# Sixteen-head causal attention: the diagonal mask moves from matmuls on TensorE to additions on VectorE

## The reference, cut to what matters

```python
q = x @ Wq;  k, v = split(x @ Wkv)             # (2, 16 heads, 1024, 16)
s = (q * 16**-0.5) @ k.T                       # (2, 16, 1024, 1024)
s = where(causal, s, very_negative)            # key <= query
out = softmax(s, axis=-1) @ v @ Wo
```

## Time and profile before

| | |
|---|---|
| time, median of 3 runs | 3386.32 us (3378.21 to 3391.15) |
| profiled execution, its own time | 3392.3 us |
| its span, first to last instruction | 3390.5 us |
| TensorE (matmul) busy | 3055.6 us, 90% |
| VectorE busy | 1947.1 us, 57% |
| ScalarE busy | 1551.8 us, 46% |
| mean granted TensorE clock | 0.944 of full speed |

### The profile page before, as it was taken

The page is one execution under the profiler, slowest core; times in us unless marked ns, Lnnn a source line. Parts: engine busy times, 40 slices in busy tenths (PEclk is TensorE's granted clock), DMA queues, the critical chain, the costliest instruction groups (busy, mean ns, idle before and its releaser), DMA issues. The chain is left out here.

```text
span 3390.5 us, 50330 instructions
## 1 busy us (share of the span) xinstructions
PE 3055.6 (90%) x17338; PEld 2117.3 (62%) x17338; DVE 1947.1 (57%) x4655; ACT 1551.8 (46%) x3708; POOL 289.9 (9%) x605
## 2 busy tenths in 40 slices
PE   7999799989999999855879999997999999959996
PEld 5555566654677777533457777775477777736764
DVE  3556455535676765785757777535477677442223
ACT  1110355542666664454446666524266666313332
POOL 0003000000011110000000000000011111002222
PEclk8998899989999999886989999998999999979998
DMA  1007433127344441010542222102734444341112
GB/s 39 19 14 161 52 47 47 14 74 222 114 140 130 145 134 46 1 29 2 156 121 80 70 82 69 41 2 74 222 117 148 120 144 136 117 145 34 33 34 90
DMA packets 233450, 293.70 MB, mean 87 GB/s; under 512 B 25502, under 2 KB 178334, under 8 KB 233073
## 3 DMA queue, kind: packets, MB, share of 16 engines
q1 hardware_dynamic: 229466, 280.39, 29.8%
q0 software_dynamic: 3744, 10.23, 1.0%
HBM read 222.01 MB, written 68.10 MB: 86 GB/s over the span
## 5 line engine op out<-in xcount | busy, mean ns | idle before, releaser
L2076 ACT ACTIVATE cond_p<-cond_p,cond_negm 128x128 f32<-128x128 f32 (+7 forms) x768 | 593.1, 775 | 419.9 <-DVE cond_negm L2107 419.2
L2057 PE MATMUL ps_o<-cond_pt,cond_v 128*64 128x256 f32 (+1 forms) x3840 | 480.5, 371 | 5.2 <-DVE attn_out L2143 0.5
L2035 PE MATMUL ps_s<-cond_k_high,cond_q_high 128*128 128x512 f32 (+3 forms) x1152 | 443.5, 391 | 15.9 <-DVE cond_negm L2107 7.7
L2107 DVE CUSTOM_DVE_ANT_0 cond_p<-ps_s,cond_side,cond_null_scores 128x128 f32<-128x128 f32 (+7 forms) x512 | 404.0, 811 | 32.2 <-PE ps_s L2037 26.1
L2037 PE MATMUL ps_s<-cond_k_both,cond_q_both 128*128 128x512 f32 (+3 forms) x1152 | 390.4, 351 | 0.0
L2047 PE MATMUL ps_t<-ident,cond_p 128*128 128x128 f32 x2304 | 350.5, 282 | 6.7 <-ACT cond_pt L2081 4.8
L2057 PEld LDWEIGHTS ps_o<-cond_pt,cond_v 128*64 128x64 f32 x3840 | 237.9, 136 | 168.5 <-issue 70.7
L2047 PEld LDWEIGHTS ps_t<-ident,cond_p 128*128 128x128 f32 x2304 | 251.0, 141 | 107.2 <-issue 78.4
L1179 ACT ACTIVATE attn_pt<-ps_t 128x512 f32<-128x512 f32 (+3 forms) x384 | 172.7, 490 | 251.3 <-PE ps_t L1140 196.8
L2035 PEld LDWEIGHTS ps_s<-cond_k_high,cond_q_high 128*128 128x128 f32 x1152 | 222.7, 193 | 49.3 <-DVE cond_negm L2107 20.1
L2115 DVE COPY cond_pt<-ps_t 128x512 f32<-128x512 f32 (+1 forms) x240 | 140.3, 585 | 167.3 <-PE ps_t L2047 165.5
(11 more groups left out here) (430 smaller groups left out, 4782.9 us busy)
## 6 DMA issues: line engine op xcount, KB each, us to landing
mqa_q_halves<-cond_q_cut SPq DMA_DIRECT2D x96, 512.0 KB, 5.8
cond_q_both<-mqa_q_halves SPq DMA_DIRECT2D x384, 128.0 KB, 3.3
cond_q_high<-mqa_q_halves SPq DMA_DIRECT2D x192, 128.0 KB, 2.9
cond_side<-in_fside_16xSxS SPq DMA_DIRECT2D x32, 512.0 KB, 7.3
moe_experts<-in_L_ffn_W SPq DMA_DIRECT2D x16, 1024.0 KB, 12.3
cond_side<-in_fside_16xSxS SPq DMA_DIRECT2D x32, 448.0 KB, 5.8
cond_side<-in_fside_16xSxS SPq DMA_DIRECT2D x32, 384.0 KB, 5.1
cond_side<-in_fside_16xSxS SPq DMA_DIRECT2D x32, 320.0 KB, 4.6
```

What stands on the lines that cost most here:

```text
L2035: nc.tensor.matmul(m.S[k % 2][:, lo:hi], c32(a.Q1[i][:, h, s * P:(s + 1) * P]), c32(a.K1[:, keys]), start=True, stop=False)
L2057: last = nc.tensor.matmul(sums[u % ON][h * HD:(h + 1) * HD, s0 * P:2 * P], a.V[:, b * QB + kb, :], PT[c % PT_SLOTS][:, (2 * h + s0) * P:(h ...
L2076: nc.scalar.activation(p, p, ACT.Exp, bias=negm[u % SMALL][:, r:r + 1], scale=-1.0, accum_out=rsum[u % SMALL][:, r:r + 1]).then_inc(exped, 1)
L2107: nc.vector.tensor_tensor_reduce(out=probs(u, r, 0, q + 1), in0=m.S[k % 2][:, 0:L], in1=toep_back(u, h, L) if cosine else a.side[h][:, SID ...
```

## The change

All mask matmuls go, in both kinds of steps. In a `max` step VectorE first reduces the columns left of the diagonal block (none for qb 0), then, for each head, adds the mask to the diagonal block and takes its negated row extreme in one instruction (`tensor_tensor_reduce`). The two parts are joined once per unit and group. In a diagonal `scores` step VectorE adds a turned mask to 128 columns in PSUM, and ScalarE waits for that (`covered`) instead of for the matmul. The `turn` step's two small instructions are plain copies, as the sign is turned before. GpSimd makes the second mask in its preamble.

```diff
@@ tensor, max step
-                            nc.tensor.matmul(out[:, at_ + lo:at_ + hi], queries, r(KS[u % 3][:, h, lo:hi]),
-                                             start=True, stop=(hi < L))
-                        last = nc.tensor.matmul(out[:, at_ + L - P:at_ + L], r(unit[:, :]), r(mask[:, :]), start=False, stop=True)
+                            last = nc.tensor.matmul(out[:, at_ + lo:at_ + hi], queries, r(KS[u % 3][:, h, lo:hi]),
+                                                    start=True, stop=True)
@@ tensor, turn step
-                    pe.wait_ge(used, maxima_until(u, G))
-                    nc.tensor.transpose(out[0:16, 0:P], mx[G][:, :], m.ident[:, :]).then_inc(made, 1)
+                    pe.wait_ge(joined, 2 * u + G + 1)
+                    nc.tensor.transpose(out[0:16, 0:P], neg_max[G][:, :], m.ident[:, :]).then_inc(made, 1)
@@ tensor, scores step
-                    if kb >= 4 * G:
-                        last = nc.tensor.matmul(out[:, s0:s0 + P], r(mask[:, :]), r(unit[:, :]), start=False, stop=True)
-                    last.then_inc(scored, 1)
@@ scalar
-                    act.wait_ge(scored, i + 1)
+                    if step in covered_of:
+                        act.wait_ge(covered, covered_of[step] + 1)
+                    else:
+                        act.wait_ge(scored, i + 1)
@@ gpsimd, preamble
+            nc.gpsimd.memset(causal_turned[:, :], 0.0).then_inc(masked, 1)
+            pool.wait_ge(masked, 3)
+            nc.gpsimd.affine_select(out=causal_turned[:, :], in_=causal_turned[:, :], compare_op=ALU.is_ge, fill=FAR,
+                                    base=0, pattern=[[1, P]], channel_multiplier=-1).then_inc(masked, 1)
@@ vector, at each diagonal scores step
+                if step in covered_of:
+                    _, u, G, kb, h = step
+                    i, s0 = score_of[step], live(G, kb)
+                    dve.wait_ge(scored, i + 1)
...
+                    block_ = m.T[i % 2][:, s0:s0 + P]
+                    nc.vector.tensor_tensor(block_, block_, causal_turned[:, :], ALU.add).then_inc(covered, 1)
@@ vector, max step
-                    L, col = (qb + 1) * P, first * 4 + qb % 4
+                    L, col, G = qb * P, first * 4 + qb % 4, qb // 4
+                    if k >= 2:
+                        dve.wait_ge(used, k - 1)
...
+                    for h in range(2 if qb < 4 else 1):
+                        if h == 1 and k >= 1:
+                            dve.wait_ge(used, k)
+                        last = nc.vector.tensor_tensor_reduce(
+                            out=diagonal[n_diagonal % 3][:, :], in0=src[:, h * GRP + L:h * GRP + L + P], in1=causal[:, :], scale=-1.0,
+                            scalar=3.0e38, op0=ALU.add, op1=ALU.min, accum_out=neg_diagonal[G][:, col + 4 * h:col + 4 * h + 1])
+                        n_diagonal += 1
+                    last.then_inc(used, 1)
+                    if step == last_max[u, G]:
+                        dve.wait_ge(used, k + 1)
+                        if u >= 1:
+                            dve.wait_ge(made, slot_of[("turn", u - 1, G)] + 1)
+                        nc.vector.scalar_tensor_tensor(neg_max[G][:, :], mx[G][:, :], -1.0, neg_diagonal[G][:, :],
+                                                       ALU.mult, ALU.min).then_inc(joined, 1)
```

More of the change, by code:

```diff
@@ L953, in stage_attn0 @@
     causal = m.sb("attn0_causal", [P, P], F32, at)
-    mask = m.sb("attn0_mask", [P, P], F32, at + 512)
-    unit = m.sb("attn0_unit", [P, P], F32, at + 1024)
+    causal_turned = m.sb("attn0_causal_turned", [P, P], F32, at + 512)
     at += 1536
@@ L960, in stage_attn0 @@
     mx = [m.sb(f"attn0_max{i}", [P, 16], F32, at + i * 64) for i in range(2)]
+    spare = m.R + 160256
+    diagonal = [m.sb(f"attn0_diagonal{i}", [P, P], F32, spare + 256 + i * 512) for i in range(3)]
+    neg_diagonal = [m.sb(f"attn0_neg_diagonal{i}", [P, 16], F32, spare + i * 64) for i in range(2)]
+    neg_max = [m.sb(f"attn0_neg_max{i}", [P, 16], F32, spare + 128 + i * 64) for i in range(2)]
     rinv = [m.sb(f"attn0_rinv{i}", [P, 16], F32, at + 128 + i * 64) for i in range(2)]
@@ L978, in stage_attn0 @@
     chunk_of = {s[1:]: i for i, s in enumerate(s for s in steps if s[0] == "attend")}
+    covered_of = {s: i for i, s in enumerate(s for s in steps if s[0] == "scores" and s[3] >= 4 * s[2])}
     r = lambda x: x.bitcast(F32R)
@@ L982, in live @@
         return max(0, kb - 4 * G) * P
-    def maxima_until(u, G):
-        return 1 + max(i for s, i in slot_of.items() if s[0] == "max" and s[1] == u and s[2] // 4 == G)
+    last_max = {}
+    for s in slots:
+        if s[0] == "max":
+            last_max[s[1], s[2] // 4] = s
     with nc.Block() as block:
@@ L1100, in _ @@
             pe.wait_ge(cleared, 9)
-            pe.wait_ge(constants, 2)
             def slot(step):
@@ L1136, in _ @@
                     out = m.T[i % 2]
-                    last = nc.tensor.matmul(out[:, s0:GRP], r(KS[u % 3][:, h, kb * P:(kb + 1) * P]), r(QS[u % 3][:, G, h, s0:GRP]),
-                                            start=True, stop=(kb < 4 * G))
-                    if kb >= 4 * G:
-                        last = nc.tensor.matmul(out[:, s0:s0 + P], r(mask[:, :]), r(unit[:, :]), start=False, stop=True)
-                    last.then_inc(scored, 1)
+                    nc.tensor.matmul(out[:, s0:GRP], r(KS[u % 3][:, h, kb * P:(kb + 1) * P]), r(QS[u % 3][:, G, h, s0:GRP]),
+                                     start=True, stop=True).then_inc(scored, 1)
                 elif step[0] == "attend":
@@ L1189, in _ @@
         def _(dve):
-            nc.vector.tensor_copy(r(unit[:, :]), m.ident[:, :]).then_inc(constants, 1)
-            dve.wait_ge(masked, 2)
-            nc.vector.tensor_copy(r(mask[:, :]), causal[:, :]).then_inc(constants, 1)
+            for G in range(2):
+                nc.vector.memset(mx[G][:, :], -3.0e38).then_inc(constants, 1)
+            n_diagonal = 0
             def halve(j):
@@ L1220, in _ @@
             for step in steps:
+                if step in covered_of:
+                    _, u, G, kb, h = step
+                    i, s0 = score_of[step], live(G, kb)
+                    dve.wait_ge(scored, i + 1)
+                    if i == 0:
+                        dve.wait_ge(masked, 4)
+                    block_ = m.T[i % 2][:, s0:s0 + P]
+                    nc.vector.tensor_tensor(block_, block_, causal_turned[:, :], ALU.add).then_inc(covered, 1)
                 if step[0] not in ("max", "turn", "den", "spread"):
```

22 lines of the change are left out of this document (11 added, 11 removed).

## The result

The changed kernel takes 3419.48 us (median of 4 runs, 3412.72 to 3424.95), the kernel before 3386.18 us (4 runs, 3378.21 to 3391.15). The ratio is 1.0097, with a 95% interval of 1.0076 to 1.0119: 33 us slower. The forecast was 3408 us within 3360 to 3448, slower by more than 0.5% being the likeliest case.

What follows compares the result with a forecast made beforehand. TensorE was taken to bound the units. 3390.5 + 20.6 (seven units) + 1 (last unit) gave 3412 us of span, 3414 of time; as the profiled execution ran 6 us above the median, 3408 us, range 3360 to 3448.

Steps and rivals of the forecast that it cites:

- a clock below 0.95: Sign set in advance: a steady unit of the changed kernel showing such a TensorE clock makes the forecast wrong.
- The handoff ring: Diagonal scores go TensorE, VectorE, ScalarE, TensorE; from an addition's start, score i+2 is ready after 1.45 us.
- +2.95 us a steady unit: Main-loop unit walked at 47.05 us: G0 17.0, G1 kb0 to kb5 25.6, kb6 and kb7 4.45; chance 0.35.
- The last unit, "about +1": Main loop's last unit, without maxima beside it: same loop through ScalarE, about +1 us, 0.4 of it in its first chunk.
- The rival that the clock falls: G0 of each unit: TensorE at 1.2 GHz, +4.4 us a unit, +31, about 3440 us; chance 0.15.
- The rival that the masks' time comes back: Additions fall into VectorE's slack; each unit 44.1 - 6.9 = 37.2 us, 3338 us in all; chance 0.18.
- The rival with nothing to see: Waits of 8 to 11 us a unit spend each side's gain, within 10 us of now; chance 0.22.
- Dearer instructions: Reducing instruction at 0.43 us makes G0 and part of G1 longer, up to 4.8 us a unit, 3442 us; chance 0.10.
- VectorE 35 us busy a unit: VectorE's work in a unit rises from 25 to 35 us, still less than TensorE's 37.2.
- The prologue hidden behind the transfer: Before the units, some 6 us more VectorE work is covered by the 14 us transfer wait; costed at nothing.
- The first unit: One of the seven main-loop units before the last, each forecast at +2.95 us.
- +20.6 and +1: Main-loop totals: +20.6 us for seven units at +2.95 each, and about +1 us for the last unit.

Runs made afterwards that it cites:

- e1: Changed kernel with the mask matmul put back into the diagonal scores, so only the maxima are masked on VectorE; 0.9997 of the kernel before.
- e2: Kernel before with only the diagonal scores masked on VectorE, the maxima keeping their mask matmuls; 1.0111 of the kernel before.
- e9: e1 plus a 128-column VectorE reduce into a spare tile at each addition's place, with no engine waiting for it; 1.0001 of the kernel before.
- e10: Kernel before, all masks kept, with diagonal exponentials waiting for a one-column VectorE copy that waits for the score; 1.0058 of the kernel before.
- e11: Changed kernel with an unread 512-column matmul behind each score matmul of the last unit only; 1.0087 of the kernel before.
- e3: Changed kernel with the 64 removed matmuls a unit put back on TensorE, multiplying zeros; 1.0123 of the kernel before.
- e13: e1 with each attend step moved ahead, right behind the chunk's fourth score; 3357.64 us, 0.9928 of the kernel before.

## Why the prediction was right, point by point

Its direction and its mechanism, the handoff, held. The time lies in a range that reached from a gain to a loss (3360 to 3448 us), so meeting it proves little. The size is part luck: one term was too high, one far too low, and the clock was left out. By its own sign ("a clock below 0.95" in a unit makes the forecast wrong) it failed in four of the six middle units, at 0.89 to 0.93.

- **The handoff ring: right.** The likeliest case said that VectorE's in-order queue between TensorE and ScalarE would give back more than the masks save. e1, e2, e9 and e10 show it from four sides. The loop was put at 1.45 us and measures 1.46. Of the 1.85 us a unit, though, the handoff alone is 1.9, and what remains is a balance of two amounts of nearly equal size: 2.7 for VectorE's work and 2.8 for the masks.
- **+2.95 us a steady unit: too high at full clock, near the truth on average.** At full clock it is +1.85. G0 was walked at 17.0 us and takes 15.84. A reducing instruction takes VectorE 0.21 to 0.22 us from start to start and not 0.27; for G0's 17 of them that would be 1 us of the difference, if none of it lay in waits. G1 kb0 to kb5 was 25.6 and is 25.40; kb6 and kb7 were 4.45 and are 4.71. Averaged over the six middle units the growth is 3.0 us (18.0 / 6), because the lower clock adds 1.1 (6.8 of the 18.0 us; 6 × 1.86 = 11.2 are the rest). That the forecast's 2.95 meets this average is chance, made of a term too high and one left out.
- **The last unit, "about +1": the step that failed.** It grew by 11.5 us. The prediction took a wait like those before it and kept the clock of 1.00 there; the clock went down to 0.69 and cost most of the growth: at least 6.7 us by e11, 9.4 if the handoff is put at e10's 2.1. With 2.1 instead of 1 the handoff was under-sized as well.
- **The rival that the clock falls (0.15): came true in part, and beside the forecast, not in its place.** It put the fall into G0 of each unit, and there most of it is, at 1.2 GHz from 508 to 514 us in the unit shown. But it came in four of six middle units, at 0.3 to 0.4 of the price given (1.5 to 1.9 us above a unit at 1.00, against 4.4 for the whole of G0 at the lower level; the fall covers only its beginning). Its largest part was the last unit, which the rival did not name.
- **The rival that the masks' time comes back (0.18): false.** It also took them too dear. 64 masks took TensorE an estimated 5 us and not 6.9 (64 x 0.11 is 7.0, to be exact), since 0.11 holds between matmuls of 128 columns only; its busy time fell by 2.8 us, where "nearly 7" was to be seen. This error is hidden in the result, since both the forecast and the truth had the saving lost under waits.
- **The rival with nothing to see (0.22): false** for the time, 33 us and not within 10, though its thought that each side's gain is spent holds for the masks and VectorE's work, −2.8 and +2.7 us a unit.
- **Dearer instructions (0.10): false.** Record 0.28 us, step 0.22, against the 0.43 of the rival. The addition's record is 0.295, taken at 0.29.
- **VectorE 35 us busy a unit: right**, 34.8 to 35.3. That its sum of work would not be the bound was right too, and e9 shows it: 6 us of work outside the ring cost a middle unit 0.0.
- **The prologue hidden behind the transfer: right as far as the runs can tell.** The maxima left 2.3 us later and the first score started 2.1 us later, where nothing was forecast, but e11 with the same prologue had it at 361.5 us, so that the difference may be one of executions.
- **The first unit** was counted as the others, +2.95. It grew by 4.6, at a clock of 0.74 against 0.81; how much of that is the clock is not separated.

In sum the forecast's +20.6 and +1 became +24 (1.3 + 4.6 + 18.0) and +11.5, and the time came out 11 us above the forecast.

What stays open: which of two units with the same steps gets the lower clock. The changed kernel has units at 1.00 and at 0.93 side by side, and with the same stops ahead of both G0 (0.69 and 0.59 us before the second pairs of kb6 and kb7). e10 kept 1.00 in all its units but the first (0.82) with the same ring, and with all masks in place; e3, which has both, fell in one middle unit and in the last. e1 and e9, without a handoff and without half of the masks, each have one middle unit at 0.96, and e13 none. That the masks' own work keeps the clock up is a guess that fits some of this, not one that was tested alone. The division of the last unit's 11.5 us is known only within the bounds above.

## What to carry to other kernels

Before moving an operation to an engine that has time to spare, look at where it stands in the ring of who waits for whom. 6 us a unit of work (33.63 against 27.38 busy) on a half-idle VectorE cost a middle unit nothing where nobody waited for it, and a copy of 0.15 us cost 1.9 us a unit (32 of them) once it stood between a score and its exponential, with two PSUM halves to turn in. With that handoff in place, 6.8 us more of VectorE's work cost 2.7 us a unit. When a small matmul is to be removed, measure its step beside the neighbours it really has; and when a change lengthens TensorE's stops, price the clock in the stretches that have no other work to fill them. Looking for work that can be moved ahead of a waiting step, as `attend` here, gave more here (2.1 us a unit) than taking 32 masks away (1.65).

## What the runs showed of the hardware that was not expected

- A mask matmul of 128 columns with its own weights takes 0.11 us of TensorE between matmuls of 128 columns, and 0.06 behind one of 512 (0.58 against 0.52 us).
- In the last unit TensorE's clock went down to 1.2 GHz with stops of 0.6 to 0.8 us ahead of a chunk's second pair of scores, and was still there when it was busy 8.00 of 9.00 us (711 to 720 us). Before, with a stop of 0.34 us at that place, it stayed at 2.4 GHz. More matmuls in the same unit made it 6.7 us shorter. But from 730 us on the clock was at 2.4 GHz with stops of up to 0.78 us, and two units with the same stops ahead of them ran one at 1.00 and one at 0.89: the length of the stops alone does not say which.
- A 128-column addition in place in PSUM took 0.295 us, and the reducing instruction with its accumulator read 0.21 to 0.22 us from start to start.
